# Attention and channel-mix kernel: the maxima's parts turned by the DMA, four operand buffers, input and attention turned in tiles of 64 rows and copied in one

## The reference

```python
xn = _layernorm(x)                                   # x: (32, 256, 128), f32
q, k, v = xn @ wq + bq, xn @ wk + bk, xn @ wv + bv   # 16 heads of 8
att = softmax(q @ k.T / sqrt(8)) @ v                 # per batch and head, 256x256 scores
a = concat_heads(att) @ wo.T + bo
x_prev = xn shifted by one token (zero in front)
xr, xk = mu_r * xn + (1 - mu_r) * x_prev, mu_k * xn + (1 - mu_k) * x_prev
f = sigmoid(xr @ W_r.T) * (square(relu(xk @ W_k.T)) @ W_v.T)
out = x + a + f
```

## Time and profile before

| | |
|---|---|
| time, median of 3 runs | 467.87 us (467.05 to 470.95) |
| profiled execution | 468.32 us, of it span 466.2 us |
| mean granted TensorE clock | 0.971 of full speed |
| busy, share of the span | PE 96%, PE weight loads 59%, DVE 86%, ACT 85%, POOL 79% |
| chain that ended last, by engine | PE 88%, DMA 3%, issue 2%, DVE 2%, ACT 2% |
| chain, by line | L631 26%, L707 18%, L717 11%, then products and turns of 1 to 5% each |
| DMA | 60.43 MB, queues busy 45% of 16 engines' span |

### The profile page before, as it was taken

How to read it: one execution, slowest core, us unless ns; L and a number is a source line. 1 busy time by engine, 2 the same in 40 slices (tenths; PEclk the granted TensorE clock), 3 DMA queues, 4 the chain that set the end, 5 groups by cost and what they waited for, 6 DMA issues and landing times.

```text
span 466.2 us, 15769 instructions
## 1 busy us (share of the span) xinstructions
PE 449.2 (96%) x5254; PEld 275.1 (59%) x5254; DVE 400.7 (86%) x824; ACT 394.1 (85%) x896; POOL 366.5 (79%) x674
## 2 busy tenths in 40 slices
PE   6689999999999999999999999999999999999996
PEld 5245666666656666556665666566656666666554
DVE  7578999999988999899999999899998999989831
ACT  2138899999988999989998999989998999989894
POOL 6667888888888988888888888888888888887321
PEclk9558999999999999999999999999999999999999
DMA  4533465545345545344554544355545444455100
GB/s 135 158 116 99 124 162 148 142 134 150 109 140 148 157 127 155 108 132 130 148 159 129 156 139 127 104 147 155 159 137 138 136 126 125 137 151 147 51 15 24
DMA packets 86061, 60.43 MB, mean 130 GB/s; under 512 B 6224, under 2 KB 73808, under 8 KB 86032
## 3 DMA queue, kind: packets, MB, share of 16 engines
q1 hardware_dynamic: 86032, 60.06, 45.0%
HBM read 29.89 MB, written 29.36 MB: 127 GB/s over the span
## 4 chain that ended last, share of the span: by engine, by line
PE 88%; DMA 3%; issue 2%; DVE 2%; ACT 2%; SPq 1%; ACTq 0%; DVEq 0%; POOL 0%
PE bank_val L631 26%; PE bank_exp L707 18%; PE bank_max L717 11%; PE misc L736 5%; PE misc L758 4%; PE misc L646 4%; PE misc L665 3%; PE misc L747 3%; PE misc L799 3%; PE misc L792 3%; PE misc L673 2%; PE misc L773 2%; PE misc L768 1%; DMA ops<-spill 1%; DVE neg_max L557 1%
## 5 line engine op out<-in xcount | busy, mean ns | idle before, releaser
L557 DVE TENSOR_REDUCE neg_max<-bank_max 128x2 f32<-128x512 f32 x512 | 327.9, 684 | 37.9 <-PE bank_max L717 32.8
L454 ACT ACTIVATE probs<-bank_exp 128x512 f32<-128x512 f32 x504 | 273.5, 597 | 27.4 <-PE bank_exp L707 25.3
L717 PE MATMUL bank_max<-ops 48*128 48x256 bf16 x1024 | 161.5, 278 | 0.0
L707 PE MATMUL bank_exp<-ops 51*128 51x256 bf16 x1008 | 156.0, 273 | 4.2 <-issue 2.1
L631 PE MATMUL bank_val<-probs,val 128*25 128x256 f32 x2048 | 136.8, 385 | 0.8 <-ACT probs L454 0.8
L707 PEld LDWEIGHTS bank_exp<-ops 51*128 51x128 bf16 x1008 | 74.7, 95 | 66.2 <-issue 51.5
L631 PEld LDWEIGHTS bank_val<-probs,val 128*25 128x25 f32 x2048 | 50.5, 103 | 52.2 <-issue 27.0
L717 PEld LDWEIGHTS bank_max<-ops 48*128 48x128 bf16 x1024 | 77.0, 96 | 5.7
L356 POOL TENSOR_SCALAR xn<-x_in,moments,rstd 128x128 f32<-128x128 f32 x62 | 49.3, 802 | 0.0
L395 POOL TENSOR_TENSOR mixed_x<-mixed_x,xn_t 128x512 f32<-128x512 f32 x32 | 40.7, 1273 | 2.5
L370 POOL TENSOR_TENSOR qk_l<-qk_rest,qk_m 128x512 bf16<-128x512 f32 x31 | 36.0, 1163 | 2.5
(11 more groups left out here) (77 smaller groups left out, 627.9 us busy)
## 6 DMA issues: line engine op xcount, KB each, us to landing
ops<-spill SPq DMA_DIRECT2D x126, 192.0 KB, 3.4
spill<-qk_h SPq DMA_DIRECT2D x64, 192.0 KB, 3.3
spill<-qk_m SPq DMA_DIRECT2D x64, 128.0 KB, 1.9
x_in<-x SPq DMA_DIRECT2D x32, 128.0 KB, 2.2
spill<-qk_l SPq DMA_DIRECT2D x32, 128.0 KB, 1.8
y_out<-y SPq DMA_DIRECT2D x32, 128.0 KB, 1.9
ops<-shift SPq DMA_DIRECT2D x128, 6.0 KB
w<-weights SPq DMA_DIRECT2D x1, 448.0 KB, 3.0
```

The costliest lines, as they stand in the source:

```text
L454: nc.scalar.activation(probs[g % 2][:, u % G, :, :], exp_bank(u, live)[:, :, :], ACT.Exp, scale=SCALE).then_inc(exp_done[u], 1)
L557: nc.vector.tensor_reduce(out=neg_max[hf][:, :, r, pr], in_=bank_max[MAX_BANK[v]][:, :, :], axis=AX_X, op=ALU.max, negate=True).then_inc(m ...
L707: exp_mm = nc.tensor.matmul(exp_bank(u, live)[:, i, :], ops[p][rows, hf, 1, pr, i * P:(i + 1) * P], ops[p][rows, hf, 0, pr, :], start=True ...
L717: max_mm = nc.tensor.matmul(bank_max[MAX_BANK[v]][:, i, :], of[rows, max_hf, 0, max_pr, i * P:(i + 1) * P], of[rows, max_hf, 1, max_pr, :] ...
```

## The change

1. The bf16 turns on TensorE and ScalarE's copy of them go. SP issues a DMA transpose from `max_parts` (now 128 columns wide for each 128 tokens, 24 used, zeroed once) to `shift`.
2. `ops` has four buffers. The operands of both halves of batch t+2 are loaded in step t. The rows of ones of the two new buffers are copied by DMA once, in step -1.
3. `xn` and `att` are turned in tiles of 64 rows, lower rows into one bank of `misc`, upper rows into the other, at neighbouring columns; one ScalarE copy takes both to `xn_t`, which is twice as wide. The bias of V goes through the output weights into `bo_all` once instead.
4. TensorE waits for `xn` and `att` ahead of the channel-mix product; at the end of unit 11 it waits for the one copy.
5. SP's order in a step becomes: transpose of half 1, spill of `qk_h`, shift load of half 1, input load, spill of `qk_m` and `qk_l`, store of batch t-2, transpose of half 0, operands of half 0, shift load of half 0, operands of half 1. GpSimd splits the maxima of half 0 ahead of `rest`.

The diff, cut to its core:

```diff
-        ops = [sb(f"ops{i}", [P, 2, 2, PR, S], BF16) for i in range(2)]
+        ops = [sb(f"ops{i}", [P, 2, 2, PR, S], BF16) for i in range(TURN)]
-        max_parts = [sb(f"max_parts{i}", [P, ST, 2, 3, PR], BF16) for i in range(2)]
-        shift = [sb(f"shift{i}", [2 * 3 * PR, S], BF16) for i in range(2)]
+        max_parts = [sb(f"max_parts{i}", [P, ST, P], BF16) for i in range(2)]
+        shift = [sb(f"shift{i}", [P, ST, P], BF16) for i in range(2)]
-        misc = [psum(f"misc{i}", [P, 2 * S]) for i in range(2)]
+        misc = psum("misc", [P, 2, 2 * S])
...
+            def copy_ones():
+                sp.wait_ge(k_filled[0], 1)
+                for i in range(2, TURN):
+                    for r in range(2):
+                        rows = slice(RG * r + KS, RG * r + KE)
+                        sp.dma_start(ops[i][rows, :, 1], ops[0][rows, :, 1]).then_inc(ones_in, 16)
...
+            def transpose_shift(half, count, before):
+                sp.wait_ge(parts_zero, 1)
+                sp.wait_ge(max_split[half], count)
+                after(sp, shift_in[half], before)
+                sp.dma_start_transpose(shift[half][:, :, :], max_parts[half][:, :, :].rearrange("p n c -> p (n c)")).then_inc(
+                    shift_done[half], 16)
...
             def step(t, c, n, moved, paired, quad, live):    # SP
-                if live(4) and live(0):
-                    sp.wait_ge(x_bo_done, n(0))
-                    sp.wait_ge(xn_done, n(0))
-                    load_x(t + 4, c)
-                if live(1):
-                    after(sp, exp_scores[H - 1], n(-1))
-                    load_ops(1, 1 - p, moved(1, SPILLS), moved(0, 2))
+                if live(0):
+                    transpose_shift(1, n(0), moved(-1, 2))
                 if live(2):
...
                     spill_part(p, "h", qk_h, h_done, n)
                 if live(0):
-                    load_shift(1, p, n(0), moved(-1, 2))
+                    load_shift(1, c, moved(0, 1), moved(-1, 2))
+                if live(4) and live(0):
+                    sp.wait_ge(x_bo_done, n(0))
+                    sp.wait_ge(xn_done, n(0))
+                    load_x(t + 4, c)
                 if live(2):
                     spill_part(p, "m", qk_m, (m_done, m_done), n)
                     spill_l(p, n)
-                    after(sp, exp_scores[HALF - 1], n(0))
+                if live(-2):
+                    store_y(t - 2, p, n(-2))
+                if live(1):
+                    transpose_shift(0, n(1), moved(0, 2))
+                if live(2):
+                    after(sp, exp_scores[H - 1], n(-1))
...
-                        load_ops(0, p, moved(2, SPILLS), moved(1, 2))
+                        load_ops(0, (c + 2) % TURN, moved(2, SPILLS), moved(1, 2))
...
-                    load_shift(0, 1 - p, n(1), moved(0, 2))
+                    load_shift(0, (c + 1) % TURN, moved(1, 1), moved(0, 2))
+                if live(2):
+                    load_ops(1, (c + 2) % TURN, moved(2, SPILLS), moved(1, 2))
+                if live(1) and not live(0):
+                    copy_ones()
...
+                    if u == 7 and (live(3) or live(-1)):     # ACT
+                        turned = xn_t[(c + 3) % TURN]
+                        after(act, ffn_psum, n(0))
+                        for r in range(2):
+                            after(act, xn_t_psum[r], n(3))
+                            after(act, att_t_psum[r], n(-1))
+                        cols = slice(0 if live(3) else S, 2 * S if live(-1) else S)
+                        nc.scalar.copy(turned[:, 1 + cols.start:1 + cols.stop].rearrange("p (n r c) -> p r n c", r=2, c=RG),
+                                       misc[:, :, S + cols.start // 2:S + cols.stop // 2].rearrange(
+                                           "p r (n c) -> p r n c", c=RG)).then_inc(xn_t_done if live(3) else att_t_done, 1)
...
-                    if u == 1 and live(0):                   # PE
-                        pe.wait_ge(max_split[1], n(0))
+                    if u == 3 and live(0):
                         pe.wait_ge(act_r_done, n(0))
                         after(pe, qk_rest_done[1], n(2))
-                        transpose_shift(1, near)
-                    if u == 3 and live(0):
-                        pe.wait_ge(shift_done[1], n(0))
...
+                    if u == 7 and live(3):
+                        pe.wait_ge(xn_done, n(3))
+                        after(pe, qk_rest_done[0], n(2))
+                        after(pe, qk_rest_done[1], n(2))
+                    if u == 7 and live(-1):
+                        pe.wait_ge(att_done, n(-1))
                     if u == 7 and live(0):
                         pe.wait_ge(act_sq_done, n(0))
                         pe.wait_ge(gate_done, n(0))
                         for i in range(ST):
                             last = nc.tensor.matmul(near[:, i * D:(i + 1) * D], act_sq[:, i * P:(i + 1) * P],
                                                     w[:, W_VV, :], start=True, stop=True)
                         last.then_inc(ffn_psum, 1)
...
                     if u == 7 and live(3):
                         for i in range(ST):
-                            last = nc.tensor.transpose(near[:, S + i * P:S + (i + 1) * P], xn[:, i, :], ident[:, :])
-                        last.then_inc(xn_t_psum, 1)
+                            for r in range(2):
+                                rows, k = slice(RG * r, RG * (r + 1)), S + i * RG
+                                last = nc.tensor.transpose(misc[:, r, k:k + RG], xn[rows, i, :], ident[rows, rows])
+                                if i == ST - 1:
+                                    last.then_inc(xn_t_psum[r], 1)
                     if u == 7 and live(-1):
-                        pe.wait_ge(att_done, n(-1))
                         for st in range(ST):
...
+                            for r in range(2):
+                                rows, k = slice(RG * r, RG * (r + 1)), S + (ST + st) * RG
+                                last = nc.tensor.transpose(misc[:, r, k:k + RG],
+                                                           att[rows, st * H:(st + 1) * H].rearrange("p k e -> p (k e)"),
+                                                           ident[rows, rows])
+                                if st == ST - 1:
+                                    last.then_inc(att_t_psum[r], 1)
...
-                    if u == 9 and live(1):
-                        pe.wait_ge(max_split[0], n(1))
...
-                        transpose_shift(0, far)
-                    if u == 11 and live(1) and live(0):
-                        pe.wait_ge(shift_done[0], n(1))
+                    if u == 11 and live(1) and live(0):
+                        if live(3):
+                            pe.wait_ge(xn_t_done, n(3))
...
```

More of the change, by code:

```diff
@@ L248, in load_first_ops, with load_shift @@
                     for r in range(2):
[L249 to L254, removed]
+                        src = spill[c % 2].rearrange("a s (e g pr) c -> g (s e) a pr c", e=E, pr=PR)[r][:, :, pairs]
+                        sp.dma_start(ops[c][RG * r:RG * r + KS, 0, :, pairs], src).then_inc(landed, 16)
+            def transpose_shift(half, count, before):
[4 more added lines that the diff above has]
+                    shift_done[half], 16)
+            def load_shift(half, c, done, before):
+                sp.wait_ge(shift_done[half], done)
                 after(sp, shift_in[half], before)
                 for r in range(2):
-                    sp.dma_start(ops[p][RG * r + KS:RG * r + KE, half, 0],
-                                 shift[half][3 * PR * r:3 * PR * (r + 1), :]).then_inc(shift_in[half], 16)
+                    sp.dma_start(ops[c][RG * r + KS:RG * r + KE, half, 0],
+                                 shift[half][3 * PR * r:3 * PR * (r + 1), :, :]).then_inc(shift_in[half], 16)
             def spill_l(p, n):
@@ L327, in split_max @@
                 m, zero = neg_max[half], zeros[:, :, :, :]
-                part = [max_parts[half][:, :, :, j, :] for j in range(3)]
+                parts = max_parts[half][:, :, 0:2 * 3 * PR].rearrange("p n (r j k) -> p n r j k", r=2, j=3)
+                part = [parts[:, :, :, j, :] for j in range(3)]
                 last_unit = HALF * (half + 1) - 1
                 after(pool, max_done[last_unit], count)
-                after(pool, shift_psum[half], before)
+                after(pool, shift_done[half], before)
                 nc.gpsimd.tensor_tensor(part[0], m[:, :, :, :], zero, ALU.add).then_inc(max_h[half], 1)
@@ L419, in _ @@
             act.wait_ge(weights_in, 16 * N_WEIGHT_DMAS)
-            def move_shift(half, bank, count, before):
-                act.wait_ge(shift_psum[half], count)
-                after(act, shift_in[half], before)
-                nc.scalar.copy(shift[half][:, :], shift_in_bank(bank)).then_inc(shift_done[half], 1)
             def move_values(parity, bank, count):
@@ L502, in _ @@
```

(9 more changed lines are left out.)

135 lines of the change are left out of this document (67 added, 68 removed).

## The result

The changed kernel takes 493.78 us (median of 4 runs, 492.73 to 498.86) against 469.41 for the kernel before, run beside it: a ratio of 1.0538, 95% interval 1.044 to 1.0637. The direction is the one forecast, the time lies above the range (465 to 491). Both wait loops that the prediction describes turned out to be there at once, and the second was longer than its sum said.

The account below looks back on a forecast made before the run. TensorE sets the 13.26 us period; waiting early for `att` makes a loop of 6.22 + 7.34 + 0.04 = 13.60. Over 29 full steps that adds 9.2 us, ends 0.3: 477 us, range 465 to 491.

Parts of the forecast that it names:

- The loop through `att`: TensorE's product waits for VectorE's `att`, which follows unit 14: period 13.60 against 13.26, +0.34 us a step.
- The DMA's turn: SP's queue from unit 14 through half 1's transpose to unit 14 again: 12.7 us, hidden under 13.60.
- L: Time from the issue of SP's DMA transpose to its landing, taken as 2.5 us.
- rival A: SP's shift loads wait for a late DMA transpose, delaying operand loads; with a 3.7 us landing about 487 us; chance 0.20.
- Ends: Prologue +0.8 us for a transpose issued ahead of the operand load, last full step -0.5: +0.3 in all.
- The bf16 turns: Two pairs at L639 leave TensorE, 0.09 us each: -0.18 us a step.
- 64-row turns: TensorE turns `xn` and `att` in 64-row pairs, taken at 0.11 us a pair: change 0, bounds -0.22 to +0.12.
- One ScalarE copy: One copy takes both turned tiles, about one exponential long, before units 8-9 reach PSUM: no cost.
- B: Rival: `att` comes in time on VectorE and TensorE's own work sets the period: 456 to 463, say 460 us; chance 0.12.
- C: Rival: turns at 0.055 us a pair and VectorE's 0.16 wait closes: period 13.22, 468 us, no change; chance 0.11.

Follow-up runs that it names:

- after: The changed kernel with the whole change, run beside the kernel before: 493.78 us, ratio 1.0538.
- e12: The changed kernel with the two waits for `qk_rest` moved from ahead of the channel-mix product to the head of unit 7: 489.47 us, ratio 1.0424.
- e4: The changed kernel with SP's order alone changed, input load first in the step and output store last: 489.77 us, ratio 1.0449.
- e11: e10 with an ordinary DMA of the same 64 KB in place of each transpose, shifts not turned: 467.16 us, ratio 0.9976.
- e5: The changed kernel with `xn` and `att` waits behind the product, before an extra turn, and SP's input load first, output store last: 478.08 us, ratio 1.0189.
- e10: e6 with the ones written by GpSimd and, in step -1 alone, half 0's operand load ahead of the first transpose: 475.81 us, ratio 1.0157.
- e6: e5 without the extra turn; `xn` and `att` awaited at unit 9, turned behind it, ScalarE's copy behind exponential 9: 478.71 us, ratio 1.02.
- e3: The changed kernel with the waits for `act_sq` and `gate` put ahead of those for `xn` and `att`: 491.23 us, ratio 1.0468.

## Why the prediction was right in direction and too low

*The loop through `att`: the mechanism right, one term mis-sized.* Terms predicted 6.22, 7.34 and 0.04 to 0.06, sum 13.60. Measured in after 6.28, 7.25 and 0.34, sum 13.87. The third failed: the release was read from the last step, where the earlier trace rows have one wait in front of a turn, and here six waits stand in the row. With the two for `qk_rest` out of it (e12) it is 0.07 and the short steps take 13.59. This term of the sum was mis-sized by 0.27 to 0.3 a step, and the 21 steady steps took 5.8 us more than forecast (12.6 for 6.8). Yet mending it (e12) brought only 4.3 us in all, because of the next point.

*The DMA's turn: the step that failed.* "Sum 10.2 + L ... I take 2.5 ... 12.7, hidden under 13.60 with 0.9 to spare." L was right: 2.45, though not for the landing alone, since the spill of `qk_h`, which the sum leaves out, keeps the queue nearly as long. The 10.2 was not: by e12's rows the rest of the way is 11.4. From unit 14 to the issue 1.48 (1.41 taken); shift loads and the gap behind them 1.77 (1.52); input load 0.47 (0.40); `qk_m` 1.01 (0.93); from the issue of `qk_l` to the operand loads 2.50 (1.87); operand loads to unit 14 4.15 (3.8); the 0.3 of gaps was taken apart from these. The largest miss is 0.63, and its cause stands in the prediction as harmless: "The half-0 turn is issued before the operand loads, which wait for `qk_l` anyway." The store and the second transpose between them take 0.39 and 1.21 with gaps, and end after `qk_l` has landed (308.18 + 1.9 to 2.0). Where the sum prices an issue of the transpose, at the start, it takes 0.8, the time of a pair of operand loads; it is 1.20, and 1.37 there.

So rival A decided from L = 2.2 (13.60 - 11.4), not from 3.4, and held together with the forecast instead of in its place. That was the second error: a chance of 0.20 for A and 0.57 for the forecast, as if one excluded the other. Nor does the second loop end where it starts, as "it ends in unit 14 again" has it: it starts at the maxima of unit 13 and closes over two steps, at 13.72 a step in e12 against 13.59 for `att`. Hence the alternation, and over the 21 steps, longer ones at loop ends among them, e12's mean is 13.87, hardly below the 13.99 of after.

*Ends: +0.3 taken, 9.7 measured* (1.1, 9.1 and 1.9, less the 2.4 of seven steps of the loop). Of the 9.4 too much, 6.7 are the seven early steps. The start had a transpose of 1.37 and its wait ahead of the load of operands, which begins at 26.26 on the chain instead of 24.05 (the earlier trace rows and above). The early steps are the SP loop's: e4, which only changes its order, brings them from 9.1 to 3.6, and e11, without the turns, to -0.4; e5 has 3.8, but 4.9 before the first `att`. The last full step should have lost 0.37 of ScalarE; it got a turn of 3.28 and a load of 1.90 instead.

*The bf16 turns.* The 0.18 a step taken off TensorE was sized rightly: in the chain of after the next unit stands right behind the mixed values (L668 at 242.27 for 0.99 and at 249.23 for 0.99, L741 at 243.26 and 250.23), where the earlier trace rows has the 0.09 of a pair. So the 0.09 that was weighed against the Trainium skill's 390 ns stood. The Trainium skill, "VectorE: DVE Perf Modes", section "Rules for kernel authors", says to turn a 128x128 tile on TensorE where PSUM will do as the destination. The runs agree with the advice: the DMA's turn costs 8.65 us more than a plain copy (e10 against e11), the four turns on TensorE 29 x 0.18 = 5.2 us at the most. The Trainium skill's 1309 ns for one square, in the same page's section "The three transpose paths", is near the 2.4 us that two took here from issue to landing.

*64-row turns: taken at no gain, in fact a small one.* All eight stand in the chain of after at 0.27 + 0.13 = 0.40, with the change of tile shape in it, against 0.44 and one more change before unit 8; some 0.15 a step. In after it doesn't reach the time, since the loop through `att` has the ScalarE copy's 0.2 on the other side (6.28 from product to unit 14, 6.22 forecast).

*One ScalarE copy: "No cost" was wrong by 0.2.* The copy takes 0.59, the exponential of unit 9 stands behind it, and unit 11 waits for that: 0.30 idle at 243.61 above. e6 only moved the wait to another unit, and e11 has it still: its turns take 0.24 where the kernel before has 0.44 and 0.18, 0.38 less, of which units 8 and 9 give back 0.27 (0.81 against 0.54). That leaves 0.11, and the period fell by 0.10.

*Rivals B and C* did not come. B needs `att` in time, and it is late in every steady step. C needs 0.22 from the turns and 0.16 on VectorE's way; the stretch from the product to unit 14 gave nothing (6.28 for 6.22), unit 14 to `att` 0.09 (7.25 for 7.34).

## What to carry to other kernels

A wait moved ahead of work that didn't need it closes a loop; its period can be read from the old trace as a sum of two stretches and a release (13.60 forecast, 13.59 measured), but the release must be read from a place with the same waits in the same order. Where a second loop is within a microsecond of the first, price its every term from rows, the issue time of a new kind of transfer above all, and add its chance to the first instead of setting one against the other. Look also at where it really starts: the loop here left from the unit ahead of the one it delayed and closed over two steps. A queue in program order hides nothing behind a wait that ends sooner than the issue put there.

## What the runs showed of the hardware

The issue of a DMA transpose of two 128x128 bf16 squares holds SP's queue for 1.20 to 1.21 us in steady steps, an ordinary copy of the same 64 KB 0.55. It lands 2.4 us after its issue in the median, but 3.28 (after) and 3.57 (e10) in the chain rows above; why these are longer stays open. With two satisfied waits taken out of a row of six, TensorE went on 0.07 us after the late one instead of 0.34 (e12 against after); with all six and the late one last it was 0.12 (e3).
